# Feed forward of a decoder layer: transposes by SyncE's DMAs, seven banks for gate and up, and other engines for roundings and subtractions

## What is computed

```python
def _act_quant(x):
    scale = 127.0 / jnp.clip(jnp.max(jnp.abs(x), axis=-1, keepdims=True), 1e-05)
    return jnp.clip(jnp.round(x * scale), -128.0, 127.0) / scale
def _bitlinear(x, w):                     # w rounded to -1, 0, 1 times its mean
    return jnp.einsum('bsi,oi->bso', _act_quant(x), _weight_quant(w))
gate = jax.nn.silu(_bitlinear(x, w_gate)) # 512 -> 2048
up = _bitlinear(x, w_up)                  # 512 -> 2048
x = _layernorm(x + _bitlinear(gate * up, w_down))  # 2048 -> 512
```

## Time and profile before

| what | us |
|---|---|
| median of 3 runs | 1814.68 |
| runs | 1810.21, 1814.68, 1814.8 |
| span of the profiled execution | 1810.6 |
| feed forward loop, period of a tile | 11.48 |

### The profile page before, as it was taken

One profiled execution on the slowest core, in us unless ns is written; L12 is line 12 of the kernel. 1 busy time (PEld: TensorE's weight loads), 2 busy tenths in 40 slices (PEclk: granted clock), 3 DMA queues, 4 the chain that ended last, 5 costly groups with the idle time before them and its releaser, 6 DMA issues.

```text
span 1810.6 us, 43108 instructions
## 1 busy us (share of the span) xinstructions
PE 1764.0 (97%) x14196; PEld 1488.3 (82%) x14213; DVE 1422.3 (79%) x3304; ACT 1182.3 (65%) x2709; POOL 1120.8 (62%) x1250
## 2 busy tenths in 40 slices
PE   8999999999998899999999999999999999989997
PEld 7777777777777899999999999889999999975553
DVE  6777778787887677777777788777777777788998
ACT  6878887756755566666666667666666665665665
POOL 3434445664566586686686655678778778552554
PEclk9999999999998999999999999999999999999999
DMA  5222223111105422432432523314313341552221
GB/s 205 76 65 91 96 81 114 43 30 43 48 21 172 136 93 95 150 98 76 150 103 70 168 92 86 112 50 123 94 60 99 95 115 48 124 110 50 70 70 64
DMA packets 107012, 166.89 MB, mean 92 GB/s; under 512 B 29900, under 2 KB 65104, under 8 KB 106944
## 3 DMA queue, kind: packets, MB, share of 16 engines
q1 hardware_dynamic: 88408, 129.75, 23.3%
q0 software_dynamic: 14656, 28.92, 5.8%
q10 hardware_dynamic: 3880, 7.35, 1.3%
HBM read 109.25 MB, written 50.46 MB: 88 GB/s over the span
## 4 chain that ended last, share of the span: by engine, by line
PE 71%; issue 10%; POOL 7%; DVE 6%; DMA 4%; ACT 2%; POOLq 0%; ACTq 0%; DVEq 0%
PE att_ps_P L1737 5%; PE att_ps_SA L1761 5%; PE att_ps_T L554 5%; PE att_ps_P L1725 4%; PE att_ps_P L1789 4%; PE att_ps_P L554 3%; PE att_ps_O L1725 3%; PE att_ps_T L1725 3%; DMA ca_ct<-ct_kept 3%; PE att_ps_T L1737 3%; PE att_ps_SB L616 3%; POOL sa_p_lo L425 3%; PE att_ps_P L1775 3%; PE att_ps_SB L602 2%; PE att_ps_O L1737 2%
## 5 line engine op out<-in xcount | busy, mean ns | idle before, releaser
L1543 POOL TENSOR_TENSOR ca_pr<-ca_pr,ca_rec 112x750 f32<-112x750 f32 x256 | 366.5, 1452 | 186.4 <-DVE ca_rec L2023 183.3
L425 POOL TENSOR_TENSOR sa_p_lo<-sa_pr,sa_p_hi 112x448 fp32r<-112x448 f32 x128 | 147.1, 1164 | 210.0 <-ACT sa_p_hi L722 209.2
L1908 ACT ACTIVATE ca_big<-att_ps_P 126x384 fp32r<-126x384 f32 (+1 forms) x254 | 105.3, 449 | 66.2 <-PE att_ps_P L1775 64.8
L1902 ACT ACTIVATE ca_pr<-att_ps_SA,ca_nmax 112x750 f32<-112x750 f32 x128 | 113.7, 888 | 21.8 <-DVE ca_nmax L2019 11.0
L891 DVE RECIPROCAL sa_sums<-sa_sums 128x224 f32<-128x224 f32 x64 | 99.1, 1548 | 34.8 <-ACT sa_sums L731 34.6
L2028 DVE TENSOR_TENSOR ca_big<-att_ps_P,ca_big 126x384 fp32r<-126x384 f32 (+1 forms) x254 | 120.0, 500 | 6.2 <-ACT ca_big L1908 5.9
L2019 DVE TENSOR_REDUCE ca_nmax<-att_ps_SA 112x1 f32<-112x752 f32 x128 | 119.2, 931 | 1.3 <-PE att_ps_SA L1761 1.2
L2019 DVE TENSOR_REDUCE ca_nmax<-att_ps_SB 112x1 f32<-112x752 f32 x128 | 119.2, 931 | 0.0
L1737 PE MATMUL att_ps_P<-ca_w_hi,ca_ct 128*126 128x256 f32 x558 | 114.1, 283 | 1.4 <-DVE ca_q_lo L2002 1.4
L1902 ACT ACTIVATE ca_pr<-att_ps_SB,ca_nmax 112x750 f32<-112x750 f32 x128 | 113.3, 885 | 0.1
L1775 PEld LDWEIGHTS att_ps_P<-att_ident,ca_pr 64*126 64x126 f32 (+1 forms) x1524 | 85.8, 138 | 14.6 <-issue 10.8
(11 more groups left out here) (355 smaller groups left out, 6688.7 us busy)
## 6 DMA issues: line engine op xcount, KB each, us to landing
ct_kept<-ca_ct SPq DMA_DIRECT2D x8, 1134.0 KB, 8.9
ca_ct<-ct_kept POOLq DMA_DIRECT2D x8, 1134.0 KB, 8.0
ct_kept<-ca_ct SPq DMA_DIRECT2D x8, 1116.0 KB, 11.5
ca_ct<-ct_kept POOLq DMA_DIRECT2D x8, 1116.0 KB, 10.4
sa_xin<-in_x_dram SPq DMA_DIRECT2D x16, 448.0 KB, 3.6
xt_kept<-ca_xt SPq DMA_DIRECT2D x8, 896.0 KB, 5.2
ca_xt<-xt_kept POOLq DMA_DIRECT2D x8, 896.0 KB, 5.0
ternary<-ca_stage SPq DMA_DIRECT2D x36, 172.0 KB, 1.9
```

The costliest lines, as they stand in the source:

```text
L425: pool.tensor_tensor(p_lo[:, h % NB, :], pr[:, h % NB, :], f32(p_hi[:, h % NB, :]), ALU.subtract).then_inc(p_split, 1)
L1543: pool.tensor_tensor(w, w, rec[:, h % PB, c:c + 1].to_broadcast([R, S]), ALU.mult).then_inc(norm_done, 1)
L1902: act.activation(pr[:, h % PB, c, :].rearrange("r (a s) -> r a s", a=2), two_halves(psum[slot]), ACT.Exp, bias=nmax[:, h % PB, c:c + 1], a ...
```

## The change

- **Transposes.** From tile 2 on `xq` is transposed by a DMA that SyncE issues (`turn_x`) into one of two `xqt`; the halves of `hq` of all tiles but the last are transposed by two DMAs (`turn_hidden`) into `hqt`. PE keeps the transposes of x for tiles 0 and 1, and of h for the last tile. SyncE's queue in the loop is: half 0 of h of t-1, load `res`, half 1 of h of t-1, load `xin`, x of t+2, each behind waits of its own.
- **Banks.** Gate and up have seven banks: up blocks 1 and 3 share one, so up block 3 of a tile waits for product 1 of the same tile; all other blocks wait for their use in the tile before. PE's order is all eight blocks of tile t, then down of t-1.
- **Roundings of x.** From tile 3 on both are on ScalarE (`round_x`, `quantise_x`), between SiLU 1 and 2, and 2 and 3; ahead of the loop they stay on VectorE.
- **VectorE.** Both last subtractions of h follow each other, directly behind the guess. The order of a tile is now: residual and statistics of t-2 (`sum_rows`), `scale_of_x(t+2)`, products 0, 1, 2, a maximum, product 3, `scale_of_hidden`, `guess_root`, the two subtractions. `scale_of_x(3)` stands ahead of product 1 of tile 1. The waits for `y_free` and `y_done` are those of before.
- Scales have a column for each tile; the loops are unrolled; `res`, `y` and `y_out` lie elsewhere; semaphores that nobody waits for share one. GpSimd's part of the feed forward is not edited.

```diff
...
-    gu_ps = [psum["SB"][:, BANK:2 * BANK], psum["T"], psum["P0"], psum["P1"]]
     first_ps = [psum["SB"][:, BANK:2 * BANK], psum["SA"][:, 0:BANK], psum["SB"][:, 0:BANK]]
+    gate_ps = [psum["SB"][:, BANK:2 * BANK], psum["P0"], psum["SA"][:, BANK:2 * BANK], psum["O"]]
+    up_ps = [psum["T"], psum["P1"], psum["SB"][:, 0:BANK], psum["P1"]]
...
+        def turn_x(t):
+            sp.wait_ge(xq_done, t + 1)
+            sp.wait_ge(up_filled, FB * (t - 1))
+            sp.dma_start_transpose(xqt[:, t % 2], xq[:, :]).then_inc(xqt_in[t % 2], 16)
+
+        def turn_hidden(t, half):
+            sp.wait_ge(hq_done[half], t + 1)
+            if half == 0:
+                sp.wait_ge(y_filled, t + 1)
+            sp.dma_start_transpose(hqt[:, half * FC // 2:(half + 1) * FC // 2, :], hq[:, half_of(half)]).then_inc(hqt_in[half], 16)
...
+            for t in range(1, T):
+                if t > 1:
+                    turn_hidden(t - 1, 0)
+                load_residual(t - 1)
+                if t > 1:
+                    turn_hidden(t - 1, 1)
+                if 4 <= t + 3 < T:
+                    load_x(t + 3)
+                if t + 2 < T:
+                    turn_x(t + 2)
+            load_residual(T - 1)
...
-                    if not first:
-                        pe.wait_ge(used, FB * t + f - 1)
+                    if not first and n == 7:
+                        pe.wait_ge(h_done, FB * t + 2)
+                    elif not first and n == 3:
+                        pe.wait_ge(h_done, FB * t)
+                    elif not first:
+                        pe.wait_ge(used, FB * (t - 1) + f + 1)
...
+        def rest():
+            pe.wait_ge(sg_done, FB)
+            for f in range(FB):
+                for ca_done in ca_free(f"v{f}"):
                     pe.wait_ge(*ca_done)
-                pe.wait_ge(held[2], 16)
-            transpose_h(t - 1, first, range(2))
-            gate_up(t, False, range(3, FB))
-            transpose_h(t - 1, first, range(2, FB))
-            down(t - 1, t + 1 if ahead else None)
-
-        def rest():
-            tile(1, first=True)
-            with pe.Fori(2, T - 1) as t:
-                tile(t)
-            tile(T - 1, ahead=False)
-            transpose_h(T - 1, False, range(FB))
+                gate_up(1, False, [f])
+            pe.wait_ge(held[2], 16)
+            down(0)
+            for t in range(2, T):
+                gate_up(t, False, range(FB))
+                down(t - 1)
+            transpose_last()
...
+        def round_x(t):
+            act.wait_ge(x_scaled, t + 1)
+            act.activation(xr[:, :], xin[:, :], ACT.Copy, scale=xscale[:, t:t + 1], bias=ROUND).then_inc(xr_done, 1)
+
+        def quantise_x(t):
+            act.wait_ge(xr_done, t + 1)
+            act.wait_ge(*before_x(t))
+            act.activation(xq[:, :], xr[:, :], ACT.Copy, bias=-ROUND).then_inc(xq_done, 1)
...
+            for t in range(1, T):
+                scale_hidden(t - 1, 0)
+                scale_hidden(t - 1, 1)
+                silu(t, 0)
+                silu(t, 1)
+                if t + 2 < T:
+                    round_x(t + 2)
+                silu(t, 2)
+                if t + 2 < T:
+                    quantise_x(t + 2)
+                silu(t, 3)
...
+        def sum_rows(t):
+            dve.wait_ge(y_free, t + 1)
+            add_residual(t, y)
+            dve.wait_ge(y_summed, t + 2)
+            dve.wait_ge(y_done, t + 1)
+            return links.mark(dve.bn_stats(stats[:, 0, :], y[:, :]))
...
-        def tile(t, statistics=True, ahead=True, ahead2=True):
-            dve.wait_ge(unit_done, t + 1)
-            hidden(t, 1)
-            if statistics:
-                dve.wait_ge(y_free, t - 1)
-                add_residual(t - 2, 1, y)
-            hidden(t, 2)
-            largest(t, 0)
-            if statistics:
-                dve.wait_ge(y_summed, t)
-                dve.wait_ge(y_done, t - 1)
-                sums = chain.mark(dve.bn_stats(stats[:, 0, :], y[:, :]))
-            hidden(t, 3)
-            if statistics:
-                chain.need(sums)
-            finish_h(t, statistics, ahead, ahead2, next_hidden=ahead)
...
+            for t in range(2, T):
+                sums = sum_rows(t - 2)
+                if t + 2 < T:
+                    scale_of_x(t + 2)
+                hidden(t, 0)
+                hidden(t, 1)
+                hidden(t, 2)
+                largest(t, 0)
+                hidden(t, 3)
+                scale_of_hidden(t)
+                guess_root(sums)
+                quantise_hidden(t, 0)
+                quantise_hidden(t, 1)
...
```

More of the change, by code:

```diff
@@ L2364, in gate_up, with transpose_last @@
                     for k in range(KC):
-                        mm = pe.matmul(gate_up_bank(f, m, first)[:, :], xqt[:, k, :], wt[m][:, k * F + f * BANK:k * F + f * BANK + BANK],
-                                       start=(k == 0), stop=(k == KC - 1))
+                        mm = pe.matmul(gate_up_bank(f, m, first)[:, :], xqt[:, t % 2, k, :],
+                                       wt[m][:, k * F + f * BANK:k * F + f * BANK + BANK], start=(k == 0), stop=(k == KC - 1))
                     mm.then_inc(done, 1)
-        def transpose_h(t, first, blocks):
-            for q in blocks:
+        def transpose_last():
+            for q in range(FB):
                 if q % 2 == 0:
-                    pe.wait_ge(hq_done, 2 * t + q // 2 + 1)
-                if not first or q >= 2:
-                    pe.wait_ge(hqt_done, FB * t + q - 1)
+                    pe.wait_ge(hq_done[q // 2], T)
+                if q >= 2:
+                    pe.wait_ge(hqt_done, q - 1)
                 for j in range(4 * q, 4 * q + 4):
@@ L2377, in transpose_h, with down @@
                 mm.then_inc(ht_filled, 1)
[L2379 removed]
+        def down(t):
             pe.wait_ge(y_summed, t + 1)
             for k in range(FC):
[L2383 to L2386 removed]
+                half = k // (FC // 2)
+                if k % (FC // 2) == 0 and t + 1 < T:
+                    pe.wait_ge(hqt_in[half], 16 * t + 16)
+                elif k % (FC // 2) == 0:
+                    pe.wait_ge(hqt_done, (half + 1) * (FB // 2))
                 mm = pe.matmul(y_ps[:, :], hqt[:, k, :], wt[2][:, k * DM:k * DM + DM], start=(k == 0), stop=(k == FC - 1))
@@ L2447, in copy_h, with silu @@
-        def copy_h(t, blocks):
-            for q in blocks:
-                act.wait_ge(ht_filled, FB * t + q + 1)
+            act.activation(xqt[:, t], xt_ps[:, :].rearrange("p (k n) -> p k n", k=KC), ACT.Copy).then_inc(xqt_done, 1)
+        def silu(t, f, first=False):
+            if f == 0:
+                act.wait_ge(x_scaled, t + 1)
+            act.wait_ge(gate_filled, FB * t + f + 1)
+            if FB * t + f >= 2:
+                act.wait_ge(h_done, FB * t + f - 1)
+            act.activation(sg[:, f % 2, :], gate_up_bank(f, 0, first)[:, :], ACT.Silu, scale=x_unit[:, t, 0:1]).then_inc(sg_done, 1)
@@ L2450, in copy_h, with copy_last @@
+        def copy_last():
+            for q in range(FB):
+                act.wait_ge(ht_filled, q + 1)
                 if q == 0:
-                    act.wait_ge(y_filled, t + 1)
+                    act.wait_ge(y_filled, T)
                 act.activation(hqt[:, 4 * q:4 * q + 4, :], ht_ps[q % 2][:, :].rearrange("p (k n) -> p k n", k=4),
                                ACT.Copy).then_inc(hqt_done, 1)
-        def scale_h(t, ahead=False):
-            act.wait_ge(hscale_done, t + 1)
-            for half in range(2):
-                if half and ahead:
-                    silu(t + 1, False, [0])
-                part_h = h[:, half * F // 2:(half + 1) * F // 2]
-                act.activation(part_h, part_h, ACT.Copy, scale=hscale[:, 0:1], bias=ROUND).then_inc(h_scaled, 1)
@@ L2667, in layers @@
         late = fixed.at + EARLY
-        mem = {"held": base, "early": fixed.at, "late": late, "rows": late + 79968, "rows_end": late + 79968 + 6144, "small": late + 95968, "ca_live": fixed.at + 34400,
+        mem = {"held": base, "early": fixed.at, "late": late, "rows": late + 79968, "rows_end": late + 79968 + 6144, "small": late + 95968, "ca_live": fixed.at + 34400, "ca_scored": fixed.at + 34400 + 7168,
                "end": nc.sbuf_base}
```

317 lines of the change are left out of this document (133 added, 184 removed).

## The result

| kernel | median, us | runs, us |
|---|---|---|
| before | 1814.74 | 1810.21 to 1816.31 |
| after | 1857.58 | 1856.94 to 1859.08 |

The forecast was 1866, with a range of 1850 to 1885.

The account below looks back on a forecast made before the run. PE bound the feed forward at 11.48 us a tile; VectorE's wait for GpSimd would make it 15.7. Tiles 45 more, start 3.2, clock 3.6: +52, 1862.6 in the profiled execution, 1866 on the median, range 1850 to 1885.

Parts of the forecast that it names:

- What the wait is: VectorE's statistics of tile t-2 wait for GpSimd's last product: 4.4 us idle in each tile from 3 to 13.
- GpSimd's chain, 7.17: Feed forward, GpSimd's subtraction to the end of its last product: 7.17 us, putting the statistics at 10.64 after product 3.
- The rest of the walk: VectorE from the statistics at 10.64 to the next product 3 at 15.7, which gives the tile's period.
- The clock term, 0.33 a tile: PE's up block 3 at 1.2 GHz after each hole: 0.33 us a tile, 3.6 in all; range 0 to 0.33.
- The transposes: DMA transposes from SyncE's queue: 3.2 us to landing for a half of h, 1.1 of it issue; covered.
- The start: Start of the loop: scale of x for tile 3 ahead of product 1 of tile 1 delays tile 2's product 3 by 3.2.
- the end: From product 3 of tile 13 to the kernel's end: same order, 17.9 us in both kernels.
- the step from the profiled execution to the median: The profiled span lies at the fast end of the runs, so 1862.6 in that execution became 1866 on the median.
- the first rival: The statistics' wait is covered after all; VectorE's period 11.3, time 1815, no change; chance 0.07.
- The case of PE at 10.37 (1800): Within the covered-wait rival: VectorE's walk also shorter, PE bound at 10.37 a tile, time 1800; chance 0.03.

Follow-up runs that it names:

- the start put back: Run with wait at the guess and scale of x behind it, plus tile 3's scale of x moved behind tile 1's scale of h: 1806.12, ratio 0.9963.
- The run with the wait at the guess: Changed kernel with one line moved: the wait for y_done stands ahead of the guess, not the row statistics; 1816.55, ratio to before 1.0015.
- one more move: Changed kernel with the y_done wait ahead of the guess, plus the scale of x, one tile further ahead, behind the guess: 1807.14, ratio 0.9963.
- four refinements: Changed kernel with four refinements of the root on GpSimd in place of three: 1875.97, ratio to before 1.0346.
- the fullest order: Changed kernel: y_done wait before guess, scale of x behind it, maximum between products 1 and 2, h halves before residual's load: 1808.63; h transposed twice: 1854.09.

## Why the forecast was right, and where its sizes were off

- **What the wait is.** As forecast: eleven waits, 4.09 each where 4.4 was worked out, released by GpSimd's last product, with PE's up block 3 idle behind product 1 (holes of 3 to 5 us) and the first subtraction waiting for ScalarE alone. Shown by taking it out, making it longer and shorter, and putting it into the kernel before.
- **GpSimd's chain, 7.17, was too long.** It measures 6.83 to 6.85 in all tiles; with the guess at 3.23 instead of 3.3 the statistics start at 10.27 instead of 10.64. The forecast allowed for this end (up to 0.9 less a tile) but took the row of before, in which VectorE's roundings of x and its two last subtractions, set apart, held GpSimd up for longer (0.90 instead of 0.57); the change takes the roundings away and puts the subtractions together.
- **The rest of the walk was short by 0.1 to 0.2.** From the statistics to product 3 it takes 5.23, not the 5.06 that lead to 15.7; the forecast's own terms add up to 5.09 to 5.12 and were rounded down. With the shorter chain the period is 15.50 instead of 15.7, and 14.29 instead of 14.5 for the last two tiles.
- **The clock term, 0.33 a tile, was mis-sized.** At block 3 the lower level came in every other tile only, and it showed in three of the eleven periods, with 0.07 each: up block 3 at that level takes 1.89, not 2.06, and product 2 (which waits 0.21 for its SiLU) and the maximum cover nearly all of it. Three stretches of 2 us at or behind block 3, and block 3 itself (columns of the first fence: busy PE, PEld, DVE, ACT, POOL; PEclk; DMA share; GB/s):

```profile
1700.00:1702.00 2.00, 2.00 (x6) 0.76 (x5) 2.00 (x3) 0.67 (x2) 0.00 (x0) 0.50 0.44 121
1714.00:1716.00 2.00, 0.99 (x5) 0.51 (x6) 1.79 (x4) 1.96 (x4) 0.00 (x0) 1.00 0.34 94
...
1732.00:1734.00 2.00, 2.00 (x6) 0.71 (x5) 1.97 (x3) 0.00 (x0) 0.00 (x0) 0.52 0.19 44
```

```profile
1715.01 1.04 PE L2420 MATMUL att_ps_P<-ff_held,ff_xqt 128*128 128x512 bf16 x4 [3.28 <-DVE ff_h L2567]
1730.51 1.89 PE L2420 MATMUL att_ps_P<-ff_held,ff_xqt 128*128 128x512 bf16 x4 [4.96 <-DVE ff_h L2567]
...
1792.67 1.89 PE L2420 MATMUL att_ps_P<-ff_held,ff_xqt 128*128 128x512 bf16 x4 [3.28 <-DVE ff_h L2567]
```

- **The transposes.** 3.2 to landing was estimated for a half of h; 3.0 is the median of 26 (2.8 to 3.7), and no matmul waited for one. The issue was taken as proportional to blocks, 1.1 for a half; it is 1.23 for 8 blocks, but 1.20 for 4 too, beside 9.10 for 64. The Trainium skill, "VectorE: DVE Perf Modes", section "The three transpose paths", lists 1309 ns for a 128x128 block; as a price per block it would make, by an estimate of 8 x 1.309, 10.5 us for a half. The trace has 3.0 us, 0.375 a block, so for small transfers too the measurement speaks against that price.
- **The start** was 3.2, and is 3.7: product 3 of tile 0 to product 3 of tile 2 is 1670.45 - 1639.91 = 30.54, and was 1667.39 - 1640.51 = 26.88. By the rows 0.99 of it comes ahead of product 3 of tile 1, 1.41 is the wait for the residual's load, and 1.26 the rest of tile 2, where 1.0, 1.2 and 1.0 were worked out. What a start without them would bring isn't shown: with the start put back the residual's add came 1.16 sooner, and product 3 of tile 2 did not.

The sum against the profiled executions: span 1856.5 - 1810.6 = 45.9 where 52 was forecast. From product 3 of tile 2 to that of tile 13 it is 1838.78 - 1670.45 = 168.33, so 43.0 more than the 125.3 before, not 48.7 (45 and 3.6 of clock); of the difference 1.8 and 0.4 are the shorter periods, and 3.4 the clock that did not come. The start adds 3.7, the end 17.7 instead of 17.9, and what lies ahead of it was 0.6 earlier. So the difference of the spans is 6 us below the sum. The other 2 to 3 between 1866 and 1857.58 lie in the step from the profiled execution to the median, for which 4 were added and which is 1.1 after the change.

The run with the wait at the guess is the case of the first rival (the wait is covered after all: 1815), at 1816.55. The case of PE at 10.37 (1800) needed one more move and came out at 1807: in that run's trace the start's price is still 3.4, and the eleven periods add up to 117.8, 3.7 more than eleven of 10.37.

## What to carry to other kernels

A wait's price depends on what stands between the event that starts the other engine and the place of the wait: before moving a step, measure the other engine's chain (here 7 us) and count the work left in between (7.7 us before, 2.9 after), even where the profile shows that wait at 0.20 us. Put a wait ahead of the first instruction that overwrites what the other engine reads, not ahead of the first that belongs to the same step: here that was one line, worth 41 us. And work taken from the busiest engine pays only once the next engine's row is shorter: the 1.12 us a tile taken from PE showed when VectorE's row had fallen from 11.45 to 10.4.

## What the runs showed of the hardware

- After the hole in front of it, up block 3 ran at 2.4 GHz or at 1.2, in turn, tile by tile, with the granted clock at 1.00 or near 0.50. In the ten tiles from 1668 to 1808 of the changed kernel, holes of 4.96 to 5.13 us were followed by the lower level (1.66 to 1.89 us for the block); after holes of 3.07, 3.28 and 3.38 the full one stayed (1.04); after 3.56 and 3.75 it was lost during or right behind the block (granted clock 0.50 from 1779 to 1781 and from 1810 to 1812); and a second hole of 3.28, above, was followed by the lower level. A tile at the lower level also shortens the next hole: from block 3 to the next tile's first block it took 5.99 us (from 1730.51) instead of 4.33 (from 1715.01). With four refinements, whose period is 16.92, block 3 took 1.89 us in each of nine tiles in a row, after holes of 3.46 to 5.07. So the length of the hole alone doesn't tell which level comes; what does stays open.
- A small DMA transpose holds SyncE's queue for some 1.2 us, whether it has 4 blocks or 8; two of them and one of x are 3.7 us a tile in that queue. Doubling those of h in the fullest order made VectorE wait 40.6 us for loads behind them.
- GpSimd's one-column operations take 0.19 us alone and up to 0.6 beside a VectorE subtraction or rounding: its chain for one and the same work was 7.17, 7.03 and 6.84 us, by what VectorE did meanwhile. In the other direction two VectorE subtractions took 1.28 us behind GpSimd's subtraction and 1.73 when begun during it.
